# A graph network's two top-2 expert stages: blocks of 256 rows one at a time, or blocks of 128 rows two at a time

## The reference

```python
# second layer: 8 experts, 256 -> 1024 -> 256 (plus one shared expert, computed elsewhere)
topw, topi = jax.lax.top_k(softmax(x @ Wr), 2)          # topw then divided by its sum
h = gelu(einsum('bsd,edf->bsef', x, W1p) + b1p)         # W1p (8, 256, 1024)
priv = einsum('bsef,efd->bsed', h, W2p) + b2p           # W2p (8, 1024, 256)
# third layer: 6 experts, 256 -> 256 -> 256 -> 256
h1 = relu(einsum('bsd,edh->bseh', x, expert_w1) + expert_b1)    # all three (6, 256, 256)
h2 = relu(einsum('bseh,ehf->bsef', h1, expert_w2) + expert_b2)
out = einsum('bsef,efo->bseo', h2, expert_w3) + expert_b3       # the two chosen, weighted, are summed
```

## Time and profile before

| | |
|---|---|
| median of three runs | 5886.6 us (5883.48 to 5891.52) |
| the profiled execution | span 5895.6 us, mean granted TensorE clock 0.861 |
| busy over the span | PE 76%, PEld 55%, DVE 57%, ACT 40%, POOL 45% |
| e3, first gather to the end of its last sum | 468.4 us, from 2646.49 |
| e5, the same | 191.2 us, from 3573.80 |
| e7, first matmul of the experts to the last sum | 237.1 us, from 5610.95 |

### The profile page before, as it was taken

How to read it: one execution, slowest core, us unless ns; L and a number is a source line. 1 busy time by engine, 2 the same in 40 slices (tenths; PEclk the granted TensorE clock), 3 DMA queues, 4 the chain that set the end, 5 groups by cost and what they waited for, 6 DMA issues and landing times. The chain is left out here.

```text
span 5895.6 us, 88327 instructions
## 1 busy us (share of the span) xinstructions
PE 4457.2 (76%) x21735; PEld 3246.9 (55%) x21840; DVE 3373.2 (57%) x6951; ACT 2387.1 (40%) x6299; POOL 2679.1 (45%) x2294
## 2 busy tenths in 40 slices
PE   5966899998794999799991957537566666474896
PEld 3433555555684999578881936423244444342486
DVE  8845788887545887500003752234699999735101
ACT  6964677775221100212330022214466565522343
POOL 4885788886114587351113703523354545200022
PEclk9987999999797999799995978758577777786998
DMA  1113555555454555106663405542244444401065
GB/s 33 12 16 106 184 195 199 200 196 173 141 189 110 138 128 158 42 13 194 191 198 107 129 31 172 164 143 77 57 138 134 135 134 134 128 21 32 0 196 168
DMA packets 431853, 724.13 MB, mean 123 GB/s; under 512 B 87458, under 2 KB 322284, under 8 KB 431180
## 3 DMA queue, kind: packets, MB, share of 16 engines
q1 hardware_dynamic: 337180, 521.50, 28.1%
q0 software_dynamic: 90000, 196.21, 12.4%
q10 hardware_dynamic: 4512, 4.46, 0.3%
HBM read 512.78 MB, written 208.45 MB: 122 GB/s over the span
## 5 line engine op out<-in xcount | busy, mean ns | idle before, releaser
L2709 POOL DMA_INDIRECT mx_at_rows<-heads,mx_at_ix x416 | 493.2, 1185 | 632.3 <-PE mx_at_pa L2755 508.8
L1272 PE MATMUL a_pa<-a_diff,a_high 128*128 128x320 f32 (+1 forms) x2000 | 609.5, 320 | 207.6 <-DVE a_low L1180 201.9
L1822 POOL DMA_INDIRECT e_xb<-table,source x188 | 181.7, 967 | 1273.4 <-issue 817.7
L1005 PE MATMUL at_pc<-at_ohr,at_ohl 128*128 128x512 bf16 (+1 forms) x3172 | 687.3, 359 | 50.9 <-DVE at_ohl L860 22.3
L782 POOL DMA_INDIRECT at_rows<-table,at_ix x416 | 579.6, 1393 | 169.5 <-issue 119.9
L967 ACT CAST y_sb<-at_pc 128x512 uint16<-128x512 f32 (+1 forms) x1092 | 519.1, 564 | 285.9 <-PE at_pc L1005 193.6
L1800 DVE TENSOR_TENSOR e_ys<-e_py,e_bl 128x256 f32<-128x256 f32 x188 | 79.9, 425 | 968.3 <-PE e_py L1749 629.2
L222 POOL DMA_INDIRECT rec_dst<-edge_rec,edge_to x400 | 557.7, 1394 | 130.6 <-issue 119.9
L1779 ACT ACTIVATE e_h<-e_phid,e_b 128x256 f32<-128x256 f32 (+1 forms) x760 | 333.2, 438 | 687.1 <-PE e_phid L1737 607.1
L1273 PE MATMUL a_pa<-a_diff,a_low 128*128 128x320 f32 (+1 forms) x2000 | 592.0, 310 | 0.0
L1737 PE MATMUL e_phid<-e_xt,e_w 128*128 128x256 f32 (+1 forms) x2800 | 524.8, 345 | 2.9 <-ACT e_xt L1767 2.9
(11 more groups left out here) (645 smaller groups left out, 8322.7 us busy)
## 6 DMA issues: line engine op xcount, KB each, us to landing
counts<-at_snap SPq DMA_DIRECT2D x157, 800.0 KB
a_cu<-counts SPq DMA_DIRECT2D x500, 160.0 KB
mx_work<-bc SPq DMA_DIRECT2D x160, 320.0 KB, 3.4
e_w<-in_L_ffn_W SPq DMA_DIRECT2D x33, 1024.0 KB
e_wl<-in_L_ffn_W SPq DMA_DIRECT2D x32, 1024.0 KB
e_wl<-in_L_ffn_Wd SPq DMA_DIRECT2D x32, 1024.0 KB
ybuf<-e_ys POOLq DMA_DIRECT2D x78, 256.0 KB
e_w<-in_L_ffn_w SPq DMA_DIRECT2D x16, 1024.0 KB
```

The costliest lines, as they stand in the source:

```text
L1005: mm = pe.matmul(pc[:, q, 0:w], ohl[:, u, j, ts(q, P)], ohr[:, u, j, 0:w], start=j == 0, stop=j == ROWS - 1)
L1272: pe.matmul(pa[:, q, 0:H], high[rows, s, ts(q // 2, P)], moving, start=s == 0, stop=False)
L2709: g.indirect_dma_start(self.rows[:, h * STEP + j, :], None, self.table, bass.IndirectOffsetOnAxis(ap=self.ix[:, h, j:j + 1], axis=0)).then ...
```

## The change

Stages e3 and e5 are now made by a new function, `expert_runs`; e1 and e7 stay as they were. The block of the two stages has 128 rows: 56 blocks in e3 and 54 in e5, in pairs, 28 and 27 turns of a loop. The routing leaves two more tables: `k.block_slot`, the expert's number modulo 2, and `k.expert_end`, the number of blocks up to an expert's end, plus 2.

SyncE loads each expert once, in order, into slot 0 or 1, and waits for all of it before it asks for the next; from the third expert on it first waits until all blocks of the expert two before have been summed. Since two blocks of a pair may belong to different experts, each engine now reads the slots of its pair from memory into registers. The weights of the hidden layers are copied inside SBUF from the slot to a fixed place `now`, one place for each block of the pair (`bring`): the first layer's by ScalarE at the end of the pair before, the later layers' by VectorE after its sums. Output weights and biases are read straight from the slot. In a pair, TensorE does layer 0 of both blocks, turns the rows of the next pair, does the other layers, and then both outputs. There are two row buffers `xb`, and GpSimd issues the two gathers of pair i+1 at the start of its turn i, behind the stores of turn i-1.

```diff
+                if kind in ("shared", "soft2"):
+                    c(v.tensor_scalar(k.block_slot[:, :], k.block_expert[:, :], 1, None, ALU.bitwise_and))
+                    c(v.tensor_scalar(k.expert_end[:, 0:EE], endb[0:1, :], 2.0, None, ALU.add))
...
+        def slots_of(eng, registers, i):
+
+            eng.load(registers, k.block_slot[0:1, ds(i * 2, 2)])
+            return [eng.snap(r, min_val=0, max_val=1) for r in registers]
+
+        def bring(eng, copy, registers, i, l):
+
+            amount, arrived = (16 * n_ld, loaded) if l else (32, first)
+            experts = [eng.value_load(k.block_expert[0:1, ds(i * 2 + s, 1)], min_val=0, max_val=E - 1) for s in range(2)]
+            slots = slots_of(eng, registers, i)
+            for s in range(2):
+                eng.wait_ge(arrived, experts[s] * amount + amount)
+                copy(now[l][:, s, :, :], ws[l][:, ds(slots[s], 1), :, :].rearrange("p a k n -> p (a k) n")).then_inc(brought[l], 1)
...
+            def _(sp):
+                for e in range(E):
+                    s = e % 2
+                    if e >= 2:
+                        released = sp.value_load(k.expert_end[0:1, e - 2:e - 1], min_val=2, max_val=nblocks + 2)
+                        sp.wait_ge(ydone, released)
+                    for q, (w, bias, _) in enumerate(hidden):
+                        arrived = loaded if q else first
+                        sp.dma_start(ws[q][:, s, :, :], w[e].rearrange("(k p) f -> p k f", p=P)).then_inc(arrived, 16)
+                        sp.dma_start(bs[q][:, s, :], bias[e]).then_inc(arrived, 16)
+                    sp.dma_start(wls[:, s, :, :], wl[e].rearrange("(k p) n -> p k n", p=P)).then_inc(loaded, 16)
+                    sp.dma_start(bls[:, s, :], bl[e].partition_broadcast(P)).then_inc(loaded, 16)
+                    sp.wait_ge(first, 32 * (e + 1))
+                    sp.wait_ge(loaded, 16 * n_ld * (e + 1))
...
+                def pair(i, more):
+                    experts = [pe.value_load(k.block_expert[0:1, ds(i * 2 + s, 1)], min_val=0, max_val=E - 1) for s in range(2)]
+                    slots = slots_of(pe, registers, i)
...
+                                pe.wait_ge(xt_copied[s], i + 1)
+                            pe.wait_ge(brought[l], i * 2 + s + 1)
+                            for f in range(ft):
+                                at = 2 * offs[l] + s * ft + f
...
+                                    mm = pe.matmul(phid[:, at % NB, 0:P], now[l][:, s, q, f * P:(f + 1) * P], src,
+                                                   start=q == 0, stop=q == kt - 1)
+                                mm.then_inc(hmul, 1)
+                        if l == 0 and more:
+                            turn_rows(i + 1)
+                    for s in range(2):
+                        pe.wait_ge(loaded, experts[s] * (16 * n_ld) + 16 * n_ld)
+                        pe.wait_ge(ydone, i * 2 + s + 1)
...
+                            mm = pe.matmul(py[:, s, 0:D], hs[-1][:, s, q, :], wls[:, ds(slots[s], 1), q, :].rearrange("p a n -> p (a n)"),
+                                           start=q == 0, stop=q == KL - 1)
+                        mm.then_inc(ymul, 1)
...
+                with pe.Fori(0, iters - 1) as i:
+                    pair(i, True)
+                pair(iters - 1, False)
...
+                def pair(i, more):
+                    slots = slots_of(a, registers, i)
...
+                        if l == 0 and more:
+                            copy_rows(i + 1)
+                    if more:
+                        bring(a, a.copy, ahead, i + 1, 0)
...
+                def outputs(i):
+                    slots = slots_of(v, registers, i)
...
+                        v.tensor_tensor(ys[:, s, :], py[:, s, 0:D], bls[:, ds(slots[s], 1), :].rearrange("p a n -> p (a n)"), ALU.add).then_inc(ydone, 1)
+
+                for l in range(1, len(dims)):
+                    bring(v, v.tensor_copy, registers, 0, l)
+                with v.Fori(0, iters - 1) as i:
+                    outputs(i)
+                    for l in range(1, len(dims)):
+                        bring(v, v.tensor_copy, registers, i + 1, l)
...
+            def _(g):
+                def fetch(B):
+                    if B >= 2:
+                        g.wait_ge(xt_done[B % 2], B // 2)
+                        g.sem_inc(passed, 1)
+                    g.indirect_dma_start(xb[:, B % 2, :], None, table,
+                                         bass.IndirectOffsetOnAxis(ap=k.source[:, B:B + 1], axis=0)).then_inc(xloaded[B % 2].sem, 16)
+
+                for B in range(2):
+                    fetch(B)
+                for B in range(nblocks):
+                    if B % 2 == 0:
+                        for n in range(B + 2, min(B + 4, nblocks)):
+                            fetch(n)
+                    g.wait_ge(ydone, B + 3)
+                    g.sem_inc(passed, 1)
+                    g.dma_start(ybuf[B * P:(B + 1) * P, :], ys[:, B % 2, :]).then_inc(stored[B % 2].sem, 16)
...
+        nb, k.experts = block_count(2 * N_NODES, 8, P), 8
+        route(nc, "r3", k, k.lg[:, :, 0:8], 8, "shared", nb, share=[a["L1_ffn_" + n][8] for n in ("W1", "b1", "W2", "b2")], second=second, columns=85, size=P)
+        expert_runs(nc, "e3", k, table, ybuf, nb, [(a["L1_ffn_W1"], a["L1_ffn_b1"], ACT.Gelu)], (a["L1_ffn_W2"], a["L1_ffn_b2"]))
+        refresh(nc, "c3", k, Gathered(ybuf[0:nb * P, :], 2), scale=k.dinv, table=table)
...
+        nb, k.experts = block_count(2 * N_NODES, 6, P), 6
+        route(nc, "r5", k, k.lg[:, :, 0:6], 6, "soft2", nb, size=P)
+        expert_runs(nc, "e5", k, table, ybuf, nb, [(a["L2_ffn_expert_w1"], a["L2_ffn_expert_b1"], ACT.Relu), (a["L2_ffn_expert_w2"], a["L2_ffn_expert_b2"], ACT.Relu)],
...
```

## The result

The changed kernel takes 5958.7 us (median of 4 runs, 5954.36 to 5974.49) where the kernel before takes 5885.0 on the same chip: a ratio of 1.0126 with an interval of 1.0111 to 1.0141, so 65 to 83 us slower. Forecast were 5952 us and +66.

A forecast was written before the change was run, and what follows sets the result against it. TensorE was taken to bound both stages before, the late gathers e5 afterwards. e3 -30 and e5 +96 gave +66 us on 5886.6: 5952 us, likeliest 5925 to 5985, 8 in 10 within 5906 to 6015.

The forecast's parts named there:

- e3, TensorE per row: Stage e3: a pair of 128-row blocks costs 14.50 us where a 256-row block cost 14.25, with 12.5% fewer rows.
- Half-clock loss: Start of e3: the first block still runs at half clock, costing 2.3 us as before.
- the mis-sized term: e3: register loads and ScalarE's work together add 0.45 us per pair, 12 us in all.
- The changes of expert: e3: next rows delayed behind an expert's 2.1 MB of weights, six times 1 us each.
- e5, the loop: e5: store, gathers, landing and remaining TensorE work close at 9.75 us, taken as 10.3 per pair for 25 pairs.
- the 0.55: e5, per pair: 0.3 us for the clock and 0.25 for VectorE, on top of the 9.75 us loop.
- e5's rim: e5 around its 25 bound pairs: start 11.4 us, first and last pairs 8 each, 2 for one expert's late weights.
- The rest: Outside e3 and e5: routing changes cancel within 1 us, later gathers read as many rows, nothing else moves.
- Gathers in time: Rival in e5: rows land in time, e5 228 us; with e3 at its best, kernel 5874 us; chance 0.06.
- VectorE delaying GpSimd's descriptors: Rival in e5: weight copies add 0.78 us per pair instead of 0.25, 13 us more, 5965 us; chance 0.2.
- Bare loads in e3: Rival: TensorE's register loads show fully in each e3 pair, 74 us more, 6026 us; chance 0.1.
- Low clock: Rival: e5's clock stays at its low level, 85 us more, 6037 us; chance 0.06.

The follow-up runs named there:

- e1: Not a follow-up run: an expert stage of the kernel, left unchanged; its first gather starts anywhere from 1530.4 to 1561.3 us over the kernels.
- e7: Not a follow-up run: the kernel's last expert stage, left unchanged, already in blocks of 128 rows, 7.25 us per 128 rows.

## Why the prediction was right, and where it was off

- *e3, TensorE per row.* 14.50 us per pair forecast from e7, 14.49 measured. Half-clock loss 2.3 forecast; the first layer took 9.59 us where later ones take 7.31. Start 11.3 forecast, 10.26 measured.
- *e3, the mis-sized term.* I had put 0.45 us per pair (12 us in all) for registers and ScalarE; it is nothing, the added loads show about 0.8 us to spare. e3 came out at 426 instead of 438. The changes of expert cost 7 us for 6, 1.8 of it at half clock.
- *e5, the loop.* 9.75 us, with 0.55 for clock and VectorE, forecast; 10.16 measured. Its parts were each a little short: gathers at 1.88 for 1.75 and 1.33 apart for 1.25, landing 2.89 for 2.75, the tail 4.10 for 3.95. That the 0.55 was near the size of these is luck: the settled pairs ran at full clock, and VectorE's copies cost a gather's issue 0.03 us (1.02 beside them, 0.99 without; 0.95 in the earlier trace rows). That the gathers, not the copies or loads, set it is shown by two edits which left those alone, the early gathers and the late transposes.
- *e5's rim.* Start 11.2 for 11.4. Changes of expert and the low clock cost more than the 2 us put there for one expert. Pairs of 10.98 and 11.17 had an expert's weights beside their gathers. The pair of 14.12 waited for such weights too, and it and one of 13.12 ran in part at half clock (second layers of 3.62 and 3.26 us for 1.95).
- *The rest.* Forecast at nothing within 1 us; it is +11, 15.4 at the two ends by GpSimd's drains, less what is gone again. So one of the prediction's own signs of being wrong, time that moves outside the two stages, came true. The e3 error of -12, this one and 3 in e5 nearly cancel: that 5952 came so near is luck. The mechanisms forecast for the two stages, fewer rows in e3 and the gather loop in e5, are what the runs show.
- *Rivals.* Gathers in time: no. VectorE delaying GpSimd's descriptors: 0.03 us of a gather's issue, 0.1 at most. The Trainium skill, page "SBUF — State Buffer", section "SBUF: two separate sides", has an exclusive lock there; no run here shows one beside these copies, which took 0.43 us each with a gather's issue beside them and without. Bare loads in e3: no. Low clock: in the changed kernel only in e5's first 52 us and near its end, in the kernel with early gathers throughout. The Trainium skill, page "TensorE: Matmul & The Clock Gate", section "HAM oscillation — how this bites in real kernels", tells of a kernel whose wait for data is longer than the work before it, and whose clock falls in each such wait; over the pairs of e5 TensorE worked longer than it waited, with the clock full (129 of 205 us) as with the clock falling (149 of 193), so no run here shows that case.

## What to carry to other kernels

Before work is reordered, follow each buffer round: from the result that frees it, over issue and landing, to the first use; where the compute between request and use is shorter than that, the round trip is the pace (6.1 us of trip hid behind 7 us of first layer in e3 and not behind 2 in e5, with the same code). Try the parts of a change apart: here a smaller block alone gave e3 its whole gain. And count a stage's price at its end too, not only in its loop.

## What the runs showed of the hardware

GpSimd's drain at a stage's end goes by the transfers it issued in the stage, gathers and stores alike: 48 in e1 3.98 us, 64 in e7 5.28, 81 and 84 with one store per pair 6.67 and 6.91, 108 and 112 after the change 8.98 and 9.20, that is 0.082 to 0.083 us each. But e3 and e5 before, with 96 and 90, drained in 1.04 and 0.63. What ended theirs early is not settled.

A higher busy share did not go with a higher clock: in e5 TensorE was busy 63% of the time at a clock of 1.00 (changed kernel) and 77% at 0.88 (early gathers, one wait of 2.1 us per pair). Nor does the pattern of the waits alone decide. Ahead of that even part, the changed kernel ran three pairs of the same loop, 10.15, 10.87 and 10.15 us long, at 0.84:

```profile
3549.53:3580.72 31.19, 23.04 (x132) 20.35 (x132) 4.89 (x12) 14.28 (x36) 9.46 (x12) 0.84 0.16 50
```

Its two pairs of 10.15 were as long as those at full clock (10.16 at the median): TensorE waits for rows there, and the low clock cost nothing. Why one stretch of the loop kept the full clock and the other didn't is open.
